# Batching the products with high x3 ahead of those with low x3, and swapping a low part with an addition in GpSimd's queue

## The reference

```python
# step 3 (input_seq = x after step 2), per batch and feature
scaling = exp(log_cumprod[:, -1:, :] - padded[:, :-1, :])       # a suffix product of the forget shares
hidden  = cumsum(scaling * new_info, axis=1) + exp(log_cumprod) * initial_hidden[:, None, :]
x = x + hidden                                                  # this is x3
# step 4
layer = base_layer[None, :, :] + einsum('bdr,bkr->bdk', x_a, x_b)   # rank 8, one per batch
out   = x + einsum('btc,bco->bto', x, layer) + x
```

## Time and profile before

| | us |
|---|---|
| median of 3 runs | 1461.57 |
| lowest, highest run | 1461.23, 1466.59 |
| the profiled execution | 1462.22 |
| its span, first to last instruction | 1460.4 |

### The profile page before, as it was taken

The page is one execution under the profiler, slowest core; times in us unless marked ns, Lnnn a source line. Parts: engine busy times, 40 slices in busy tenths (PEclk is TensorE's granted clock), DMA queues, the critical chain, the costliest instruction groups (busy, mean ns, idle before and its releaser), DMA issues. The chain is left out here.

```text
span 1460.4 us, 49898 instructions
## 1 busy us (share of the span) xinstructions
PE 1424.0 (98%) x21213; PEld 1128.5 (77%) x21213; DVE 993.7 (68%) x2706; ACT 661.0 (45%) x2200; POOL 690.4 (47%) x555
## 2 busy tenths in 40 slices
PE   7889999999999999999999999999999998899998
PEld 6568888888888888888888888888887777577776
DVE  5445767676767676767676767676756679998894
ACT  4444454545454545454545454545444443333332
POOL 3442434343434343434343434343434436778774
PEclk9899999999999999999999999999999999999999
DMA  9750333333333333333333333333324557989994
GB/s 375 274 206 6 60 60 60 60 60 60 60 60 60 60 60 60 60 60 60 60 60 60 60 60 60 60 60 60 53 39 96 143 106 126 285 319 330 335 330 146
DMA packets 442337, 168.16 MB, mean 115 GB/s; under 512 B 406481, under 2 KB 409681, under 8 KB 438914
## 3 DMA queue, kind: packets, MB, share of 16 engines
q1 hardware_dynamic: 441584, 164.53, 44.6%
q10 hardware_dynamic: 530, 0.44, 0.1%
HBM read 96.78 MB, written 68.16 MB: 113 GB/s over the span
## 5 line engine op out<-in xcount | busy, mean ns | idle before, releaser
L464 PEld LDWEIGHTS recb<-hs,scanS 128*128 128x128 f16 x16384 | 444.2, 96 | 161.4 <-DVE hs L1278 157.4
L464 PE MATMUL recb<-hs,scanS 128*128 128x32 f16 x16384 | 494.8, 177 | 14.8 <-DVE hs L1278 11.9
L699 ACT ACTIVATE hs<-pre 128x64 f16<-128x64 f32 x512 | 132.1, 258 | 611.4 <-DVE pre L1269 609.5
L1269 DVE TENSOR_REDUCE pre<-recb 128x64 f32<-128x128 f32 x512 | 149.5, 292 | 339.6 <-PE recb L464 339.5
L1122 DVE RECIPROCAL gates<-gates 128x64 f32<-128x64 f32 (+1 forms) x484 | 257.9, 555 | 0.4
L951 POOL TENSOR_TENSOR xt<-xt,hbuf 128x512 f32<-128x512 f32 (+1 forms) x65 | 99.2, 1526 | 170.7 <-ACT hbuf L703 170.7
L939 POOL TENSOR_TENSOR x1lo<-xt,x1hi 128x512 fp32r<-128x512 f32 x64 | 82.7, 1294 | 185.7 <-ACT x1hi L709 185.7
L957 POOL TENSOR_TENSOR gates<-gates 128x512 f32<-128x512 f32 x62 | 80.0, 1290 | 168.0 <-DVE gates L1122 168.0
L1278 DVE TENSOR_TENSOR hs<-konst,hs 128x64 f16<-128x64 f32 x512 | 104.0, 203 | 70.6 <-ACT konst L700 70.6
L964 POOL TENSOR_TENSOR xt<-xt,pout 128x512 f32<-128x512 f32 x64 | 76.0, 1187 | 150.5 <-DVE pout L1148 150.5
L1158 DVE TENSOR_TENSOR recb<-xw,recb 128x128 f32<-128x128 f32 x512 | 146.1, 285 | 0.0
(11 more groups left out here) (225 smaller groups left out, 2756.6 us busy)
## 6 DMA issues: line engine op xcount, KB each, us to landing
xt<-in_x SPq DMA_DIRECT2D x64, 256.0 KB, 3.6
g_d<-gst SPq DMA_DIRECT2D x64, 256.0 KB, 3.8
n_d<-nst SPq DMA_DIRECT2D x64, 256.0 KB, 3.0
x_d<-xt SPq DMA_DIRECT2D x64, 256.0 KB, 3.1
out<-gates SPq DMA_DIRECT2D x63, 256.0 KB, 6.4
xt<-x_d SPq DMA_DIRECT2D x28, 512.0 KB, 4.8
stage<-in_w SPq DMA_DIRECT2D x11, 1024.0 KB, 6.6
xt<-g_d SPq DMA_DIRECT2D x14, 512.0 KB, 7.1
```

Of the source, the lines that this page charges most:

```text
L464: last = nc.tensor.matmul(sums[t % 2][:, m].rearrange("p a b -> p (a b)"), w[:, k, m * P:(m + 1) * P], hs[:, k].rearrange("p a b -> p (a b ...
L699: nc.scalar.activation(hs[:, :, 0, :], pre[t % 2][:], ACT.Tanh, scale=unscale).then_inc(s_h, 1)
L1269: nc.vector.tensor_reduce(pre[t % 2][:], sums[t % 2].rearrange("p c a b -> p c b a"), axis=AX.X, op=ALU.add).then_inc(s_pre, 1)
```

## The change

TensorE does the same products. Within a chunk the eight with high x3 now come first, quarter by quarter, and then the four with low x3. The wait for low x3 (s_x3l) moves from the head of the chunk to between the two. The waits for a quarter's bank stay with its first product. In GpSimd's queue x3_low(2) and add_P(last, 3) change places.

```diff
             def chunk_products(b, m):
                 q = b % 2
                 pe.wait_ge(s_x3h, C * b + m + 1)
-                pe.wait_ge(s_x3l, C * b + m + 1)
                 for t in range(NT):
                     ...
-                    tok = slice(t * P, (t + 1) * P)
-                    for e, (x3, w) in enumerate(((x3hi, bhi), (x3lo, bhi), (x3hi, blo))):
-                        last = nc.tensor.matmul(quarter(b, t)[:], x3[q][:, m, tok], w[:, m, :], start=(m == 0 and e == 0), stop=False)
+                    for w in (bhi, blo):
+                        nc.tensor.matmul(quarter(b, t)[:], x3hi[q][:, m, t * P:(t + 1) * P], w[:, m, :], start=(m == 0 and w is bhi), stop=False)
+                pe.wait_ge(s_x3l, C * b + m + 1)
+                for t in range(NT):
+                    last = nc.tensor.matmul(quarter(b, t)[:], x3lo[q][:, m, t * P:(t + 1) * P], bhi[:, m, :], start=False, stop=False)
                 last.then_inc(s_pm, 1)
...
             times_n(3)
+            x3_low(2)
             add_P(last, 3)
-            x3_low(2)
             x3_low(3)
```

## The result

| | before | after |
|---|---|---|
| median of 9 runs each, us | 1462.0 | 1472.19 |
| lowest, highest, us | 1461.23, 1466.59 | 1467.38, 1472.68 |
| span of the profiled execution, us | 1460.4 | 1470.6 |

The ratio is 1.0049, 95% interval 1.0031 to 1.0066: slower, and the interval lies wholly above 1. The forecast was 1465.6 us in a range to 1468.6, so the median lies outside it. The executions of either kernel fall on two levels, some 5 us apart, and the two medians come from different levels; their own ratio, 1.0070, takes in that distance too.

A forecast was written before the change was run, and what follows sets the result against it. GpSimd's queue was taken to set the time up to 1271.2 us, TensorE after it. Profiled execution 1462.22 + 0.4 (clock) + 3.6 (banks) = 1466.2 us, against the runs' median 1465.6 us; range 1461.3 to 1468.6 us.

The forecast's parts named there:

- Sum: Whole kernel: profiled execution 1462.22 us + 0.4 + 3.6 = 1466.2 us; against the runs' median 1461.57, forecast 1465.6 us, + 0.27%.
- exchange in GpSimd's queue: Up to 1271.2 us: x3_low(2) runs while add_P(15, 3) would wait; cost 0 to 0.02 us, taken as 0, no gain.
- slow first y products: At 1254.8 us: lower clock after a longer TensorE gap slows batch 0's y products; 0 to 0.7 us, taken as 0.4.
- banks: Chunk 0 of each batch: fewer products before quarter 1's PSUM bank wait; 0.28 us at each of 14 boundaries, 3.9 us.
- gap at 1363.15 us: TensorE's existing 0.48 us gap, from a chain of transfers, absorbs one boundary's loss, leaving 13 x 0.28 = 3.6 us.
- clock behind the second y products: From 1271.2 us, where TensorE bounds: no low-clock loss in the sum; rival D alone added 1.5 us beyond the cover.
- rival D: Bank restarts 14 x 0.46 = 6.4 us, lower clock to 1271 us adding 0.7 + 1.5: 1470.2 us; chance 0.09.
- head: Everything up to the last product of the gates: no instruction changed there, and the sum gave it no term.
- early lead: Up to 1271.2 us: new product order puts TensorE some 4 us ahead, lost waiting for y_low(0); worth 0.
- A: Second of two products on one stationary operand goes faster, 213 ns instead of 227: 3.4 us, 1462.2 us; chance 0.09.
- C: Banks hide it: ScalarE's copies release sooner than read, so the pass over the banks costs nothing: 1462 us; chance 0.08.
- B: Early lead is kept as GpSimd or ScalarE move up; 3.75 us kept gives 1461.9 us; chance 0.06.

The follow-up runs named there:

- e2: The kernel before with only x3_low(2) and add_P(last, 3) exchanged in GpSimd's queue, products unchanged; ratio to before 1.0004, tail 229.03 us.
- e3: Changed kernel, but chunk 0 of batches 1 to 15 goes quarter by quarter with three products, as before; ratio to before 1.0023, batch 13.05 us.
- e9: The changed kernel again, unaltered, beside the kernel before on another chip or at another hour; ratio to before 1.0057, tail 232.84 us.
- e7: Changed kernel plus 5 added products, results unread, ahead of the wait for the second y products alone; ratio to before 1.0028, tail 232.94 us.
- e5: Changed kernel, but in chunk 0 of batches 1 to 15 the first quarter gets its three products together; ratio to before 1.0011, batch 13.13 us.
- e8: Changed kernel with chunk 0 of batches 1 to 15 by quarters and y_low(0) ahead of times_n(6) on GpSimd; ratio to before 1.0023, tail 227.69 us.
- e10: e3's products except batch 1 wholly in new order; y_low(0), y_low(1), y_high(1) and batch 1's output copies moved earlier; ratio to before 0.9999, tail 228.49 us.
- e11: e10's places in GpSimd's and ScalarE's queues, but all products by quarters as before; ratio to before 1.0012, tail 228.86 us.
- e12: e8 plus added products, results unread: 11 ahead of batch 1's chunk 0, 6 ahead of the second y products; ratio to before 1.0009, tail 229.52 us.
- e4: Changed kernel, but batch 0 goes quarter by quarter as before; ratio to before 1.0046, tail 234.79 us.
- e1: Changed kernel without the exchange in GpSimd's queue, so only the products in new order; ratio to before 1.0049, tail 234.26 us.
- e6: Changed kernel plus added products, results unread: 14 ahead of the first y products' wait, 5 ahead of the second's; ratio to before 1.0024, tail 232.82 us.

## Why the prediction was wrong

**The sum.** The step that failed is the one under "Sum", 1462.22 + 0.4 + 3.6 us: it took the head for granted and left the second fall of the clock out. In the two profiles the 10.2 us divide as follows:

| term | forecast | measured | shown by |
|---|---|---|---|
| exchange in GpSimd's queue, by itself | 0 | 0.0 | e2: first y products at 23.42 us, before 23.48 |
| slow first y products | 0.4 | 0.47, in some executions 0 | y1: 16.87 against 16.40 |
| banks | 3.9 | 4.2 | 14 x 0.30; e3 takes it away |
| gap at 1363.15 us | -0.3 | -0.55 | in before's profile, absent in e2 and e3 too |
| clock behind the second y products | 0 (1.5 in rival D) | 1.5, in some executions 0 | in the first profile, not in the second (e9), nor in e7 with the gap filled |
| head | 0 | 4.55 | same instructions; e9 and before's 110 executions |

**The head.** The largest miss, and it was in front of me: of the three runs shown one was 1466.59 us against 1461.23 and 1461.57. I treated the sum's base as exact to 0.7 us, where another execution of the same kernel is 5 us away. Had I added that level with its share, the range would have gone to 1472 us or more. The traces show the slow rate in TensorE: between two steps of the recurrence six products stand, and they took 1.45 and 1.48 us in turn in before's trace and 1.48 every time in the changed kernel's, at a granted clock of 1.00 in both. Why an execution takes the one or the other is open; no run here was made for it.

**The banks.** The mechanism and its size were right: 0.28 us a boundary forecast, 0.29 to 0.30 measured, with the load's wait where it was said to be. e5 shows its two parts, 0.22 and 0.08 us; I had 0.23 and 0.05. That the net of 3.65 us comes out so near my 3.6 is luck: I let the gap at 1363.15 us cover one boundary, 0.28 us, but e2, e3, e8, e10, e11 and e12 have nothing to cover at that place and no gap either. It was a late transfer in the one execution shown, and its whole 0.55 us fell away.

**The clock.** The first fall came as forecast, but its cause was ascribed wrongly: I put the early lead down to the new order of the products, and e2 and e4 show that the exchange makes the gap without them; e1 shows that they make it without the exchange, 4.10 us. My bounds for the slow y products were right in kind: 0 where the clock falls behind them, as the prediction read it off the first 0.8 us behind the gap of 3.88 us (e1, e5, e7, e9), and 0.47 where it falls ahead of them (the changed kernel, e2, e3, e4). That the first profile gave the 0.4 I took is partly luck. The cover for the slow chunks 4 and 5 held: 16.87 us, nothing beyond the late start. What I did not ask is whether TensorE, now ahead in batch 1, would have another gap at the second y products, where nothing covers a low clock: it was 0.87 us before and 1.51 after. I had read the danger off gaps of 3 us and more, and 1.51 us was enough. Only rival D had a price for it, tied to a restart at each bank that did not come.

**The rivals.** A and C are excluded by e3 and by the boundary's rows, B by the first y products at 23.45 us after the tail's start. D had the right price for a low clock behind the second y products, 1.5 us, and was wrong in its first part, 0.30 us a boundary and not 0.46. The Trainium skill (TensorE: Matmul & The Clock Gate, "Step-by-step: what each phase is for") says that with the load apart from the multiply one load can serve many products. These kernels load for every product all the same, 21213 loads in both, and two products on one stationary operand gain nothing here by standing together: 13.05 us a batch in e3 as before.

## What to carry to other kernels

Where a buffer comes free a fixed time after the last one, what matters is how much work stands ahead of the wait, not how much stands in all: reordering that takes one product of 0.23 us from there costs 0.23 us at every boundary if the engine is the bound. A lead that ends at the same wait buys only a longer gap, and a gap, here one of 1.5 us, can cost the clock for the work behind it; price it wherever the engine has no slack behind the gap. And look at the scatter of the runs before a sum is set against one of them: two levels in three runs belong in the range.

## What the runs showed of the hardware

The recurrence, with the same instructions and the same granted clock of 1.00, runs at one of two rates that hold from the second block to the last: 72.96 us a block in eight of the fourteen profiles and 73.38 or 73.39 in six, 5 to 6 us in all.

In the tails of the fourteen profiles TensorE stood idle 27 times for 2.23 us or more, and the granted clock went to 0.50 each time, at the earliest 2.2 us ahead of the end of the idle time and at the latest 1.94 us behind it. Seven gaps were 1.37 to 2.07 us long. Behind four of them it fell, 1.33 to 2.21 us after their end (1.51 us in the changed kernel, 1.74 in e1, 1.37 in e4, 1.72 in e5), and behind three it did not (1.44 in e9, 1.60 in e6, 2.07 in e8). Behind gaps of up to 1.25 us it never did. So a gap of 1.5 us in the same kernel costs the clock in one execution and not in another, and what decides it is not its length alone. With the first wait filled by products of 512 columns whose result nobody reads (e6, e12) the clock stayed at 2.4 GHz behind it, where all ten profiles with 3.03 us or more of idle time ahead of the first y products or of the chunk behind them had a fall. For the second (e7) one profile is weak evidence, since e9 had none there either; the totals of the executions are the better one.

A weight load whose wait ends late starts together with its product, and the next product follows 0.31 to 0.35 us later instead of 0.227 (1292.48 and 1292.83 us in the changed kernel). A wait of 0.2 us on a load hides below the product in flight but for 0.02 to 0.05 us.
